# Two-layer cross-attention and FFN kernel: the offset stage's tail in another order on TensorE and ACT, and idle TensorE products in it and behind the last output product

## The reference

```
x = x + autocorrelation_attention(norm(x), ctx)   # 16 heads, FFT correlation, top 4 lags, rolled values
x = x + frequency_ffn(norm(x))                    # FFT, sparse weights, inverse FFT
x = x + sampled_attention(norm(x), ctx)
x = x + quantised_ffn(norm(x))                    # 16-bit activations, 4-bit weights, sigmoid gate
```

```
off  = norm(x) @ w_off + b_off            # per token, head and point (16 heads x 4 points): 2 offsets
attw = softmax(norm(x) @ w_attw + b_attw) # over the 4 points
v    = ctx @ w_value + b_value
out  = sum over points of attw * (linear interpolation of v at the position that the offset gives)
x    = x + out @ w_out + b_out
```

## Time and profile before

| | |
|---|---|
| median of 3 runs | 1006.85 us (1002.65 to 1007.42) |
| the profiled execution | 1004.41 us, of which its span is 1002.6 us |
| mean granted TensorE clock of the span | 0.932 |
| PE busy | 838.5 us (84%) |
| DVE, ACT, POOL busy | 684.9, 539.4, 306.0 us |

### The profile page before, as it was taken

One profiled execution on the slowest core, in us unless ns is written; L12 is line 12 of the kernel. 1 busy time (PEld: TensorE's weight loads), 2 busy tenths in 40 slices (PEclk: granted clock), 3 DMA queues, 4 the chain that ended last, 5 costly groups with the idle time before them and its releaser, 6 DMA issues.

```text
span 1002.6 us, 12939 instructions
## 1 busy us (share of the span) xinstructions
PE 838.5 (84%) x4501; PEld 539.6 (54%) x4501; DVE 684.9 (68%) x1237; ACT 539.4 (54%) x1009; POOL 306.0 (31%) x236
## 2 busy tenths in 40 slices
PE   4999998799999998788888899599998994005998
PEld 3776675577777886244444444344443441004887
DVE  2567767866775676579888888735534999895333
ACT  2444434455334665666666666134428995982432
POOL 2100000566110222587777778200010431000000
PEclk9999999799999999599999999799998997556999
DMA  9800000010000000000000000000002436710111
GB/s 290 256 1 1 1 1 1 0 55 0 2 11 1 1 1 1 0 2 1 1 1 1 2 1 2 1 0 1 0 1 84 168 146 275 262 71 11 53 52 53
DMA packets 23446, 45.41 MB, mean 45 GB/s; under 512 B 2323, under 2 KB 18646, under 8 KB 22230
## 3 DMA queue, kind: packets, MB, share of 16 engines
q1 hardware_dynamic: 21776, 43.08, 12.1%
q10 hardware_dynamic: 1606, 1.52, 0.5%
HBM read 27.80 MB, written 16.78 MB: 44 GB/s over the span
## 4 chain that ended last, share of the span: by engine, by line
PE 60%; DVE 20%; POOL 8%; ACT 6%; issue 5%; ACTq 1%; DMA 0%; DVEq 0%; POOLq 0%
PE pair L1313 8%; PE pair L1272 8%; POOL hat L596 5%; PE pair L967 5%; PE pair L1194 4%; PE pair L1075 3%; PE pair L1102 3%; PE pair L1208 3%; PE pair L971 3%; DVE peak L1758 2%; DVE wide L1753 2%; DVE peak L1743 2%; DVE wide L1781 2%; PE pair L1012 2%; PE pair L1104 2%
## 5 line engine op out<-in xcount | busy, mean ns | idle before, releaser
L596 POOL TENSOR_TENSOR hat<-hat 128x1024 f32<-128x1024 f32 x62 | 145.6, 2360 | 45.1 <-DVE hat L1619 44.4
L1178 PE MATMUL pair<-rows,sel 32*128 32x512 bf16 x256 | 75.4, 397 | 23.1 <-ACT down_b L816 17.3
L1619 DVE SCALAR_TENSOR_TENSOR hat<-pair,down_a 128x1024 f32<-128x1024 f32 x64 | 78.1, 1220 | 21.8 <-PE pair L1170 19.7
L1297 PE MATMUL pair<-xqs,wuT 128*128 128x512 f32 x192 | 85.9, 610 | 4.8 <-ACT up_stage L861 4.8
L816 ACT ACTIVATE down_b<-pair 128x512 f32<-128x512 f32 x128 | 69.4, 595 | 37.0 <-PE pair L1178 32.1
L816 ACT ACTIVATE down_a<-pair 128x512 f32<-128x512 f32 x128 | 69.5, 595 | 33.5 <-PE pair L1178 24.0
L1313 PE MATMUL pair<-wdT,hid 128*128 128x256 f32 x384 | 84.8, 384 | 2.9 <-DVE hid L1800 2.9
L1619 DVE SCALAR_TENSOR_TENSOR hat<-pair,down_b 128x1024 f32<-128x1024 f32 x64 | 78.0, 1219 | 11.9 <-PE pair L1170 11.7
L1272 PE MATMUL pair<-xqs,wgT 128*128 128x512 f32 x192 | 85.1, 601 | 0.0
L1313 PEld LDWEIGHTS pair<-wdT,hid 128*128 128x128 f32 x384 | 74.1, 193 | 13.5 <-DVE hid L1800 3.2
L513 POOL TENSOR_TENSOR rstd<-lnt,half 128x8 f32<-128x8 f32 (+2 forms) x15 | 26.5, 1769 | 167.5 <-DVE lnt L1354 167.5
(11 more groups left out here) (208 smaller groups left out, 1880.8 us busy)
## 6 DMA issues: line engine op xcount, KB each, us to landing
up_far<-up_stage SPq DMA_DIRECT2D x24, 512.0 KB, 2.6
ups<-up_far SPq DMA_DIRECT2D x8, 1536.0 KB, 6.7
x_sb<-in_x_dram SPq DMA_DIRECT2D x8, 512.0 KB, 8.2
c_sb<-in_ctx_dram SPq DMA_DIRECT2D x8, 512.0 KB, 9.0
out_dram<-x_sb SPq DMA_DIRECT2D x16, 256.0 KB, 2.1
four<-in_c_four_dram SPq DMA_DIRECT2D x1, 1280.0 KB, 5.7
deq<-in_L_ffn_w_gate_dram SPq DMA_DIRECT2D x1, 768.0 KB, 6.8
deq<-in_L_ffn_w_up_dram SPq DMA_DIRECT2D x1, 768.0 KB, 8.5
```

The lines of the kernel that those rows point to most:

```text
L596: nc.gpsimd.tensor_tensor(hat[:, n % RING, :], hat[:, (n - 2) % RING, :], hat[:, n % RING, :], ALU.add).then_inc(summed, 1)
L1178: mm(bank[6 + i], sel[g:g + 32, pp, 1, :], rows[g:g + 32, q, c * 2 + a, :], start=True, stop=True).then_inc(down_mm, 1)
L1297: last = mm(bank[2 + oc], wuT[:, c, oc * 128:(oc + 1) * 128], xqs[:, t % 2, c, :], start=(c == 0), stop=(c == DC - 1))
L1619: V.scalar_tensor_tensor(hat[:, n % RING, :], pair[n % 2][:].rearrange("p i t -> p (i t)"), 0.0, down[n % 2][:].rearrange("p i t -> p (i t ...
```

## The change

ACT takes the exponent before the copy of the rows where both fall in one tick, and the first two `keep_v63` move from tick 129 to tick 131, behind `second_part(6)`. PE takes `turn_parts(5)` before the four `values63`. A helper `keep_busy(n, place)` issues n products of the bf16 identity with 512 columns of `rows` (written long before) into a bank whose content nobody reads: 6 and 10 of them around `turn_w63` (with waits for the last `keep_v`), 6 behind `turn_parts(7)`, and 24 behind the last output product, after a wait for the last `hat`, ahead of the wait for `attT_copied` and of `spread_peak(0)`.

```
 # ACT
                 nth(t, S5 + 1, keep_v)
-                if t == S5 + B + 1:
+                for tick, step in ((2, exponent), (10, keep_rows), (7, second_part), (5, first_part)):
+                    if group_at(t, tick) is not None:
+                        step(group_at(t, tick))
+                if t == S5 + B + 3:
                     keep_v63(0)
                     keep_v63(1)
-                for tick, step in ((10, keep_rows), (7, second_part), (2, exponent), (5, first_part)):
-                    if group_at(t, tick) is not None:
-                        step(group_at(t, tick))
 # PE
+            def keep_busy(n, place):
+                for _ in range(n):
+                    mm(place, idn16[:], rows[:, 0, 0, :], start=True, stop=True)
...
                 nth(t, S5 + 1, project3)
+                if t == S5 + B + 6:
+                    pe.wait_ge(v_kept, B)
+                    pe.wait_ge(off_kept, B)
+                    keep_busy(6, bank[3])
+                    turn_w63()
+                    keep_busy(10, bank[3])
+                if group_at(t, 9) is not None:
+                    turn_parts(group_at(t, 9))
                 if t == S5 + B + 1:
                     for p in range(NQ // 2):
                         values63(p)
-                if t == S5 + B + 6:
-                    turn_w63()
-                if group_at(t, 9) is not None:
-                    turn_parts(group_at(t, 9))
+            keep_busy(6, bank[3])
...
             project_att(NQ - 1, 1)
 
+            pe.wait_ge(hat_done, PAIRS)
+            keep_busy(24, bank[3])
             pe.wait_ge(attT_copied, 2 * NQ)
```

## The result

The changed kernel takes 1000.09 us in the median of 20 runs, against 1007.16 for the kernel before in runs on the same chip: the ratio is 0.9945, with a 95% interval of 0.9932 to 0.9958, so about 5.5 us faster. The forecast was 1001.2.

The account below looks back on a forecast made before the run. The prediction took a serial chain in the offset stage's tail and TensorE's clock, there and at the seam, as limits. Tail 5.1, sampling's start 0.2 and seam 0.3 sum to 5.6 us off the median 1006.85: 1001.2, range 997.3 to 1004.8.

Parts of the forecast that it names:

- Steps 1 to 5 of the tail: Offset stage's tail: the new order followed instruction by instruction, sampling beginning at 405.0 instead of 410.14, 5.1 us earlier.
- The price of an idle product: Idle products in tail and seam: 0.22 us each at full clock, costing the tail 0 to 0.1 us.
- The two other sides of the bound: Dearer idle products: at 0.27 us the tail's ten cost 0.5 and the seam's 24 0.3; at 0.44, 2.2 and 4.4.
- Sampling's start: Sampling's first pairs: the clock falls again within them, only the first products gain, 0.2 us; bounds -0.5 to 2.2.
- the rival: Sampling: the clock stays up, gaining 2.2 us there, 7.6 in all, 999.2 us; chance 0.25.
- The seam: Behind the last output product: 24 idle products gain 0.3 us, the clock most likely falling before 652; bounds -0.7 to 2.0.
- The clock holds from 424 on: Sampling's steady state: the clock holds with the same small products between takes, said for the clock staying up, chance 0.25.
- The spread of the runs, "likely by when the clock moves": Whole kernel before: its runs spread over 4.8 us, likely by when the clock moves.

Follow-up runs that it names:

- order_only: The changed kernel's new order on TensorE and ACT without any idle products; ratio 0.9975 to the kernel before, with an interval that goes past 1.
- warm_pairs: The changed kernel plus two more idle products behind the down products of each of sampling's first four pairs; ratio 0.9950 to the kernel before.
- no_seam: The changed kernel without the 24 idle products behind the last output product; its ratio to the kernel before is that of the changed kernel.
- slack_seam: Changed kernel with fillers in sampling's first four pairs and TensorE's slack, plus fillers at the seam; median 1.1 us from that of the same kernel without seam fillers.
- hold1: The changed kernel plus one idle product of 128 rows ahead of every odd sampling pair's up products; lost 5.3 us to the changed kernel by the ratios.
- hold_thin: The changed kernel plus two 32-row idle products ahead of every odd sampling pair's up products; eight of ten runs from 1009.9 to 1019.9 us, two at 1036.6.
- the three slack kernels: Changed kernel with fillers in sampling's first pairs and slack (median 999.26 us), then also at the seam, then also before the last stage (ratio 0.9903 to before).
- idle_only: The order of the kernel before with all idle products of the change; ratio 1.0026 to the kernel before, with an interval that just includes 1.
- before_hold: The kernel before plus two 128-row idle products ahead of every odd sampling pair's up products; median 6.7 us slower than the changed kernel with the same fillers.
- hold2: The changed kernel plus two 128-row idle products ahead of every odd sampling pair's up products; lost 8 us to the changed kernel by the ratios.

## Why the prediction was right

The median came out 1.1 us below the forecast and inside the range. As a ratio the forecast was 1001.2 / 1006.85 = 0.9944, against 0.9945 measured. That it is so close is luck: the interval is 1.3 us to either side, and the two traces differ by 6.2. By its steps:

- *Steps 1 to 5 of the tail* (5.1 us): measured 5.24. The trace came 0.4 later to the tail; with that taken off, first_part(6) started at 390.5 (forecast 390.65), turn_parts(5) at 390.2 (390.25), the coefficients of group 7 ended at 397.2 (397.3), turn_parts(7) started at 402.4 (402.45), sampling at 404.9 (405.0). The chain was followed instruction by instruction with durations from rows, and it held because the one stretched instruction beside POOL came again. One reading was off and did no harm: two of group 7's instructions on DVE ran ahead of the copy before too (391.17 and 391.61). order_only shows that 4.4 of it is the order's.
- *The price of an idle product*, 0.22: measured 5.13 for 23 and 2.32 for ten. Each set ended before, or within 0.05 of, what waited for PE. The two other sides of the bound (0.27, 0.44) did not occur.
- *Sampling's start* (0.2): the mechanism, a fall within the first pairs, is what the trace shows, at 410.0. The size was 0.56, by two terms: 0.36 at the small products, for which I had 0.2 here and 0.4 in the rival, and 0.2 behind the first take, since the clock came back 11.6 us after sampling's start instead of 13.0. warm_pairs gives the price of the rival: against the kernel before, its second take is 14.00 - 11.30 = 2.7 us sooner, fillers included, where I had 2.2.
- *The seam* (0.3): 0.40 in this pair of traces, 0.15 to 0.65 over all, and 0.24 more in the gate product that no_seam has without the products. The fall before the gate product came as said; slack_seam shows that the work between had to be filled too.
- *"The clock holds from 424 on"* was true of the one trace and wrong of most variants: it fell after the first pairs in warm_pairs, hold1, hold_thin and the three slack kernels, and stayed down far past them in order_only and idle_only. I gave the sentence in support of a rival and did not count with its failure. Half clock in sampling, at 0.3 us per us, moved one execution by 12.8 us (order_only), more than all the change does. I had bounded the effect on sampling at -0.5. The forecast was of a median, and the median happened to move with the traces.
- *The spread of the runs, "likely by when the clock moves"*, is only in part sampling's. Most runs of the kernel before have the same mean granted clock, 0.932, and still lie from 1002.3 to 1007.7. The traces show two other places, both ahead of the tail, where the code is the same in all thirteen. In five of the thirteen, TensorE's first products are slow for longer, and all that follows is 2.2 to 2.8 us later than in the trace of the kernel before (the rows print a clock of 1.00 at that time in both). And behind an idle time of 2.6 us near 193 the clock fell in ten of the thirteen and not in the three others, which is worth 1.6. Below are a row each of before and before_hold, and one each of before and hold2:

```profile
18.72 0.61 PE L951 MATMUL pair<-big,c_sb 128*128 128x128 f32 x4
19.71 1.06 PE L951 MATMUL pair<-big,c_sb 128*128 128x128 f32 x4
195.00:196.00 1.00, 1.00 (x6) 0.55 (x4) 1.00 (x5) 0.26 (x1) 0.58 (x1) 0.50 0.00 0
195.00:196.00 1.00, 1.00 (x8) 0.73 (x7) 1.00 (x4) 0.46 (x2) 0.37 (x2) 1.00 0.00 0
```

The traces of before and of the changed kernel went the same way at both places, so the account of the two is not touched by this. The medians of single kernels with 6 to 12 runs are.

The Trainium skill (TensorE: Matmul & The Clock Gate, Why this matters for your kernels) advises against idle gaps between bursts of matmuls. The traces show that this doesn't suffice here. The clock fell at 410.0 in the changed kernel and at 428.8 and 462.9 in warm_pairs, and in the five microseconds before each of these falls PE had no idle time over 0.64 us. hold2 and hold_thin differ by the rows of their fillers alone. In the first pairs PE was also less busy (0.74) than later, and no run varies there the one without the other.

What stays open is why the clock stays down for 50 us in one execution and for 7 in another. None of the 52 runs of the kernels with fillers of 128 rows along sampling (hold2, hold1, before_hold and the three slack kernels) lies over 6.4 us above the fastest of its kernel, while order_only spreads over 31 us, hold_thin over 27 and warm_pairs over 17. But no_seam, without such fillers, spreads over 6.6 only, and the traces don't show it: the changed kernel had 6.8 us at half clock, hold2 10.2. Nor was the moment of the fall against the pairs varied.

## What to carry to other kernels

Where an engine that works in order has a copy ahead of a link of the serial chain, move the copy behind it, and follow the chain instruction by instruction: here that gave 4.4 us, and the forecast of the whole tail was right to within 0.2. Idle products that keep TensorE's clock up belong only under waits that are there anyway: 128 of them, some on a path where TensorE is the bound, cost 7.5 us, more than the clock gave back. Read the granted clock of more than one execution before you trust a stretch of it. A change of 0.5% is smaller than what the clock does by chance, so compare many runs, and if idle products are added, compare also with the same ones in the kernel before.

## What the runs showed that was not expected

- With products of 32 rows alone and PE busy 0.74 of 5 us, the clock fell (405 to 410 in the changed kernel). In order_only it stayed at half for the first 50.8 us of sampling, with PE busy 0.95 of them.
- In sampling a microsecond at half clock costs 0.3 us, not 0.5: two pairs take 4.21 us instead of 2.92, as ACT and DVE hold a part of the path.
- The clock came back under six idle products at half clock (2.31 us for the six), so in this trace the fall ended under them. In the kernel before, without them, the clock stayed at half from 399.3 to 423.2.
- In the first 20 us the row of the clock says 1.00, while four products take 1.06 us in one trace and 0.61 in another: there the products tell the rate, and the row doesn't.
